# Gate logits of a mixture-of-experts block: token tiles as the stationary operand, 16 gate columns streamed

## The reference, cut to what matters

```
h = layernorm(x) * (1 + ca) + sa
x = x + ga * attention(h)
h = layernorm(x) * (1 + cb) + sb
logits = einsum('bsd,ed->bse', h, gate_w)          # 32 x 512 x 16, contraction over 256
scores = softmax(logits, axis=-1).transpose(0, 2, 1)
topk_w, topk_idx = top_k(scores, 64)                # each expert takes 64 tokens
out = scatter_add(experts(h[topk_idx]) * topk_w) + shared(h)
x = x + gb * out
```

## Time and profile before

| | before |
|---|---|
| median of three runs | 2378.26 us (2375.6 to 2378.57) |
| the profiled execution | 2380.66 us, span 2378.6 us |
| PE busy, share of the span | 94% |
| DVE, ACT, POOL busy | 70%, 49%, 62% |
| granted clock of PE, mean over the span | 0.989 of full |

### The profile page before, as it was taken

The page is one execution under the profiler, slowest core; times in us unless marked ns, Lnnn a source line. Parts: engine busy times, 40 slices in busy tenths (PEclk is TensorE's granted clock), DMA queues, the critical chain, the costliest instruction groups (busy, mean ns, idle before and its releaser), DMA issues.

```text
span 2378.6 us, 40049 instructions
## 1 busy us (share of the span) xinstructions
PE 2233.8 (94%) x13432; PEld 1954.5 (82%) x13432; DVE 1660.2 (70%) x3117; ACT 1158.4 (49%) x2138; POOL 1470.9 (62%) x1156
## 2 busy tenths in 40 slices
PE   5799999999999999999989999999999999999997
PEld 4688888888788878888878888888888888888886
DVE  6788888999999999999765554545555554554543
ACT  4566666667666666566443333333333333333332
POOL 3666666666766766766545666666666666666664
PEclk8899999999999999999999999999999999999999
DMA  3212112122122112112154443444443444443433
GB/s 100 72 57 74 71 64 76 65 70 75 58 74 80 57 68 84 58 69 75 55 124 83 87 86 59 87 90 83 89 87 58 85 89 83 88 88 58 86 62 45
DMA packets 83202, 179.59 MB, mean 76 GB/s; under 512 B 12320, under 2 KB 47296, under 8 KB 83072
## 3 DMA queue, kind: packets, MB, share of 16 engines
q0 software_dynamic: 49152, 67.14, 17.7%
q1 hardware_dynamic: 33600, 109.98, 13.6%
q10 hardware_dynamic: 320, 0.56, 0.1%
HBM read 110.29 MB, written 67.34 MB: 75 GB/s over the span
## 4 chain that ended last, share of the span: by engine, by line
PE 57%; POOL 20%; issue 12%; DVE 7%; ACT 3%; DMA 1%; POOLq 0%; DVEq 0%; ACTq 0%; SPq 0%
PE ps L385 17%; PE ps L386 17%; PE ps L387 17%; DVE stage L1071 3%; POOL x_rows L1397 3%; POOL v_f L1356 3%; POOL weights L1374 3%; POOL v_f L1362 3%; POOL hidden L1341 2%; PE ps L538 2%; PE ps L473 1%; POOL rstd L1350 1%; POOL out_factor L1427 1%; PE ps L426 1%; ACT weights L716 1%
## 5 line engine op out<-in xcount | busy, mean ns | idle before, releaser
L385 PE MATMUL ps<-x_t,weights 128*128 128x512 f32 x1536 | 611.3, 398 | 11.1 <-DVE hidden_f L1305 4.2
L1441 POOL DMA_INDIRECT out<-x_rows,step_token x256 | 418.4, 1634 | 324.0 <-DVE x_rows L1285 265.2
L386 PE MATMUL ps<-x_t,weights 128*128 128x512 f32 x1536 | 600.9, 391 | 0.0
L387 PE MATMUL ps<-x_t,weights 128*128 128x512 f32 x1536 | 599.6, 390 | 0.0
L385 PE MATMUL ps<-weights,hidden 128*128 128x256 f32 x2048 | 585.2, 286 | 4.9 <-DVE hidden L1312 2.3
L386 PE MATMUL ps<-weights,hidden 128*128 128x256 f32 x2048 | 580.6, 284 | 0.0
L387 PE MATMUL ps<-weights,hidden 128*128 128x256 f32 x2048 | 580.5, 283 | 0.0
L1305 DVE TENSOR_TENSOR hidden_f<-gelu,ps 128x512 f32<-128x512 f32 x256 | 175.6, 686 | 385.8 <-ACT gelu L868 385.8
L868 ACT ACTIVATE gelu<-ps 128x512 f32<-128x512 f32 x256 | 152.4, 595 | 551.6 <-PE ps L387 551.6
L385 PEld LDWEIGHTS ps<-weights,hidden 128*128 128x128 f32 x2048 | 393.3, 192 | 15.5 <-issue 2.9
L386 PEld LDWEIGHTS ps<-weights,hidden 128*128 128x128 f32 x2048 | 393.5, 192 | 7.3
(11 more groups left out here) (160 smaller groups left out, 3838.2 us busy)
## 6 DMA issues: line engine op xcount, KB each, us to landing
pairs<-mod_rows SPq DMA_DIRECT2D x36, 512.0 KB, 3.7
x_rows<-in_x SPq DMA_DIRECT2D x32, 512.0 KB, 3.5
h_rows<-stage SPq DMA_DIRECT2D x32, 512.0 KB, 2.6
out<-y_rows SPq DMA_DIRECT2D x32, 512.0 KB, 2.8
value_mods<-value_rows SPq DMA_DIRECT2D x32, 384.0 KB, 3.4
stage<-in_wg SPq DMA_DIRECT2D x16, 512.0 KB, 3.6
stage<-in_wd SPq DMA_DIRECT2D x16, 512.0 KB, 6.2
stage<-in_wu SPq DMA_DIRECT2D x16, 512.0 KB, 4.9
```

Source lines behind the costliest of these rows:

```text
L385: pe.matmul(o, lhs(HI), rhs(HI), start=start, stop=False)
L386: pe.matmul(o, lhs(HI), rhs(LO), start=False, stop=False)
L387: return pe.matmul(o, lhs(LO), rhs(HI), start=False, stop=stop)
L1441: pool.indirect_dma_start(out=out_rows, out_offset=bass.IndirectOffsetOnAxis(ap=ICUR[g][:, t:t + 1], axis=0), in_=X1[:, g % 2, t * D:(t + ...
```

## The change

`gate` now holds a tile of 128 tokens still and streams the 16 gate columns. For each of four token tiles it issues six matmuls (2 halves by 3 parts) that accumulate in the 16 columns of PSUM bank 3 where the transposed logits stood before. The two waits for the split operands stand once at the front, for both halves. `gate_copy`, `gate_transposes`, the SBUF tile `gate_logits_t` and two semaphores are gone, and `gate_max` waits for `gate_done`.

```
             def gate(n):
                 if at(n, 0):
                     pe.wait_ge(gw_ready, 1)
-                for k in range(KD):
-                    wait(pe, h2t_hi, n * KD + k + 1)
-                    wait(pe, h2t_lo, n * KD + k + 1)
-                    mm = mm3(PC[0:E, 2 * S:3 * S], lambda a: GW[:, a, k, :], lambda a: H2_T[:, a, k, :],
-                             k == 0, k == KD - 1)
+                wait(pe, h2t_hi, (n + 1) * KD)
+                wait(pe, h2t_lo, (n + 1) * KD)
+                for t in range(T):
+                    for k in range(KD):
+                        mm = mm3(PC[:, 3 * S + t * E:3 * S + (t + 1) * E],
+                                 lambda a: H2_T[:, a, k, t * P:(t + 1) * P], lambda a: GW[:, a, k, :],
+                                 k == 0, k == KD - 1)
                 mm.then_inc(gate_done, 1)
-
-            def gate_transposes(n):
-                wait_apart(pe, gate_read, n + 1)
-                for t in range(T):
-                    mm = pe.transpose(PC[:, 3 * S + t * E:3 * S + (t + 1) * E], GLT[:, t * P:(t + 1) * P],
-                                      IDENT[0:E, 0:E])
-                mm.then_inc(gate_t_done, 1)
...
                     gate(i - 1)
-                    gate_transposes(i - 1)
...
-            def gate_copy(n):
-                act.wait_ge(gate_done, n + 1)
-                wait(act, gate_t_done, n)
-                act.copy(GLT[:, :], PC[0:E, 2 * S:3 * S]).then_inc(gate_read, 1)
-
...
                     gelu(i - 1, 1)
-                    gate_copy(i - 1)
                     hidden_hi(i - 1, 1)
...
             def gate_max(n):
-                dve.wait_ge(gate_t_done, n + 1)
+                dve.wait_ge(gate_done, n + 1)
```

More of the change, by code:

```diff
@@ L136, in block_kernel @@
         GMX = sb("gate_max", [P, T])
-        GLT = sb("gate_logits_t", [E, S])
         GL = sb("gate_logits", [P, T, E])
@@ L184, in block_kernel @@
         h2t_done, h2t_hi, h2t_lo = map(sem, ("h2t_done", "h2t_hi", "h2t_lo"))
-        gate_done, gate_read, gate_t_done, gmax_ready, gl_ready, gexp_done, gsum, grs, sg_ready = map(
-            sem, ("gate_done", "gate_read", "gate_t_done", "gmax_ready", "gl_ready", "gexp_done", "gsum", "grs", "sg_ready"))
+        gate_done, gmax_ready, gl_ready, gexp_done, gsum, grs, sg_ready = map(
+            sem, ("gate_done", "gmax_ready", "gl_ready", "gexp_done", "gsum", "grs", "sg_ready"))
         gu_done, gelu_done, mul_done, hid_hi, hid_lo, hid3_lo = map(
```

## The result

The change made the kernel slower: 2417.8 us (median of 4 runs, 2414.93 to 2420.09) against 2378.14 us for the kernel before, a ratio of 1.0171 (95% interval 1.0159 to 1.0184). That is 39.7 us where I had forecast 1.7 us the other way; the time lies far outside my range.

A forecast was written before the change was run, and what follows sets the result against it. PE, busy 94%, was taken to bound the kernel, with DVE's queue second. Gains of 1.1 us without a round and 0.3 to 1.0 with one, taken as 1.7: 2378.26 - 1.7 = 2376.6 us, range 2372.5 to 2385.0.

The forecast's parts named there:

- the sum on PE: At the gate on PE: 24 short matmuls at 0.110 us replace the old 2.73 us piece, gaining 0.09 us per sequence.
- the last sentence: Sign of being wrong: the granted clock falls in these stretches; at 1.2 GHz the 24 loads would take twice as long.
- its floor: Skill page's floor between starts of short matmuls, about 25 ns; 24 would take 0.6 us, not used as it omits loads.
- The pace: Step between the 24 gate matmuls on PE, set by exposed weight loads: taken as 0.110 us, forecast range 0.107 to 0.114.
- The first rival (0.120): Gate step on PE is 0.120 us, `gate_max` about 0.25 later; costs 5.8 us, 2384.1 in all; chance 0.22.
- the second (0.061): Rival: gate step as short transpositions, 0.061 us; PE saves 1.27 us, in full in 12 iterations; 2362 us; chance 0.05.
- the fourth (0.213): Rival: gate step 0.213 us, 2.4 us more in nearly all 32 iterations, 2454 us; chance 0.02.
- DVE: On DVE, `gate_max` late by 0.00 to 0.04 us; slack 0.03 or 0.09 us in iterations with one round.
- ACT: The 0.57 us copy goes, but `hidden_hi` of chunk 1 waits for DVE's product anyway; nothing counted.
- The loop through PE, with DVE as second way: Phase A loop closes through PE, so gate savings count per iteration until DVE's queue into `hidden3_lo` is later.
- the third rival: PE's gain is hidden entirely, the wait at 870.95 being slack after all; gain 0, 2378.3 us; chance 0.08.
- The forecast sum, with the clock held: Total gain over phase A: 1.2 to 2.1 us, taken as 1.7, for 2376.6 us; phase B untouched.

The follow-up runs named there:

- 32 columns: The change with each of the 24 gate matmuls streaming its 16 gate columns twice, 32 in all; 2412.9 us (1 run).
- the variant with 128 columns: The change with each of the 24 gate matmuls streaming its 16 gate columns eight times, 128 in all; 2376.4 us, 0.9988 of the kernel before.
- 8 wide matmuls: The change with only the gate's high-by-high part, 8 matmuls instead of 24, each streaming 128 columns; 2417.18 us, ratio 1.0154.
- variants with 64 and 128 columns: The change with 16 gate columns repeated to 64 or 128 per gate matmul; 2378.8 us (1 run) and 2376.4 us (11 runs).
- the kernel with the split gate: Kernel before, logits' transpositions moved between the halves of `gate_up` 2, `gate_max` behind the round; 2403.66 us, or 2382.95 with filler matmuls.

## Why the prediction was wrong, point by point

- **The step that failed** is the sum on PE, "24 x 0.110 = 2.64 us in place of 2.73": it priced what stands behind the gate at the full clock, unchanged. The runs showed 1.62 us more per fall in 26 sequences. I did name the clock, in the last sentence, as something that would make me wrong, but gave it no place among the rivals, no price and no chance. What I named there, 24 loads at half speed, isn't what happened either: they ran at 0.112 us and the full clock at nearly every gate, and the fall came behind them. It should have been the rival on the slower side. One fall costs about half its length (1.62 us of 3.4), and how long one can be stands in the trace of the kernel before, in its setup, where PE's clock is at the lower level for 3.4 us and longer:

```profile
55.00:58.40 3.40, 3.40 (x10) 2.61 (x9) 2.17 (x7) 0.00 (x0) 1.01 (x1) 0.50 0.00 0
```

- **What I could have seen.** The kernel before streams 512 columns in each of its six gate matmuls; the change streams 24 x 16 = 384 columns in the same 2.7 us instead of 3072. I worked out that 16 columns add no time to a load, and didn't ask what else they stand for. The busy share says nothing on it.
- **The rule.** The Trainium skill says of this in "TensorE: Matmul & The Clock Gate" (section "What's actually happening") that the clock gate sets PE's clock by how busy the array was of late. The runs agree, once busy isn't read as the profile's busy share, which was full ahead of the fall: at one and the same pace of matmuls, 32 columns gave 0.51 in the stretch behind the gate and 64 gave 1.00. I had cited this page for its load time and for its floor, and passed over the part that spoke against the change.
- **The pace** was right: 0.110 forecast, 0.112 measured. The gain on PE was still only half of mine, 0.04 us per sequence instead of 0.09, as 24 steps turn 0.002 us into 0.05. The first rival (0.120) and the second (0.061) didn't occur, nor the fourth (0.213).
- **DVE**: `gate_max` late by 0.04 us, as forecast. That such lateness reaches the loop in iterations with a round was right in kind, and shown by moving `gate_max` in the variant with 128 columns (where it is 0.09 us late); in number it was 4 of those iterations and not all 16.
- **ACT**: the copy's removal brought nothing that the end depends on; `hidden_hi` of chunk 1 stands where it did in most iterations and up to 0.09 us earlier in others; in two (gates 2 and 30) it starts 1.55 instead of 2.07 us behind the gate, since DVE's product is ready early there and the copy had stood in the way.
- **The loop through PE, with DVE as second way** was right: 0.5 us less per iteration without a round with 8 wide matmuls, and a longer wait ahead of line 473's transpositions in those with one. So the third rival, a gain hidden entirely, is out too.
- **The second rival's price** was wrong, though it didn't occur. A much faster gate would not have brought 1.27 us per iteration but 0.5, since `gate_up` 2 waits for the product of chunk 1 until 2.17 us. I never asked whether what stood behind the gate could start earlier.
- **The forecast sum, with the clock held**, can be checked with the 128-column variant: it is the change as I had costed it. It came out 0.12% faster, 2.9 us (0.7 to 5.0), where I had 1.7. That is in part luck: the two traces show 0.05 us less per iteration without a round instead of 0.09, and some 0.7 us less in the loop as a whole once its one fall is set aside. The rest lies behind the last gate, where the traces of before and of the variants with 64 and 128 columns spread from 1174.7 to 1181.5 us without an edit.

## What to carry to other kernels

Where many short matmuls replace a few long ones at equal time, count the columns that stream, not the busy time; if they drop, look for the clock behind that place, iteration by iteration, and if loads are exposed anyway, fill their shadow by streaming the operand several times over into unused columns. Before a piece of PE work is made shorter, look for the wait that it covers: time saved turns into idle time at the next wait, and that can cost the clock as well. A few matmuls that nobody reads, in a wait that can't be avoided, may be the cheapest cure.

Of all versions tried, the change with 128 streamed columns is the fastest, 0.9988 of the kernel before (0.9979 to 0.9997); the one with `gate_max` moved as well, 0.9991 (0.9982 to 1.0), can't be told from it.

## What the runs showed of the hardware that I had not expected

- A waste of columns was free under a load: 128 columns instead of 16 per matmul left the pace at 0.112 us and the time 41 us lower.
- Idle time was neither needed for a fall nor always followed by one. 24 short matmuls without any idle time lowered the clock; 1.18 us of it behind 8 wide matmuls left the clock alone (gate at 268.97). Ahead of the eight transpositions, waits of 1.60 to 1.74 us were never followed by a fall in the loop, and longer ones sometimes: 1.79, 1.82 and 2.17 us (507.06) were, 1.81 us in the same kernel as the 1.82 wasn't, nor was 2.37 us in the kernel with the split gate.
- The row of a short matmul can start before its weights are in. The second of the gate starts 0.03 us behind the first (126.64, 126.67) and lasts 0.26 us instead of 0.17, while its load starts only with the first matmul; the steps are to be read from the loads or from later rows:

```profile
126.64 0.19 PEld L385 LDWEIGHTS ps<-gate_w,x_t 128*128 128x128 f32 x1
```

- Which of the 32 gates kept the clock has an order. Counted from 0, the distance from gate to fall shrinks from 3.57 us at gate 1 to 2.68 at gate 9, and gate 10 has no fall; then from 3.69 to 2.29, and gate 19 has none; then from 3.62 to 2.30, and gate 27 has none. The other three without one are gates 0, 30 and 31. So it goes with the time at which a gate comes, not with its instructions, which are the same. Why stays open; no experiment was made on that.
